# Keeping split expert weights on chip between the two expert stages of a macaron block

## What is computed

```
x = L0_attn_x
x = x + 0.5 * ffn(layernorm(x), router, gate, up, down)
x = x + attention(layernorm(x), W_qkv, W_out)      # rotary, causal, 16 heads
x = x + 0.5 * ffn(layernorm(x), router, gate, up, down)

ffn(x):   top 2 of 8 experts by x @ router.T, their logits through a softmax
          out = sum over the two e of weight_e * (silu(x @ gate[e].T) * (x @ up[e].T)) @ down[e].T
```

## Time and profile before

| | |
|---|---|
| median of 3 runs | 1350.76 us (1350.12 to 1356.05) |
| the profiled execution | 1353.68 us, its span 1351.6 us, mean granted clock 0.956 |
| f1 routing block | about 6 to 51 us |
| f1 expert block and attention | 51 to about 1059 us |
| f2 routing block | about 1060 to 1104 us |
| f2 expert block and final sum | 1104 to 1352 us |

### The profile page before, as it was taken

How to read it: one execution, slowest core, us unless ns; L and a number is a source line. 1 busy time by engine, 2 the same in 40 slices (tenths; PEclk the granted TensorE clock), 3 DMA queues, 4 the chain that set the end, 5 groups by cost and what they waited for, 6 DMA issues and landing times. The chain is left out here.

```text
span 1351.6 us, 27022 instructions
## 1 busy us (share of the span) xinstructions
PE 1232.3 (91%) x8148; PEld 906.6 (67%) x8148; DVE 934.7 (69%) x2002; ACT 785.9 (58%) x2230; POOL 848.0 (63%) x911
## 2 busy tenths in 40 slices
PE   7699999938999999999999999999998879999990
PEld 6488888825666666666666666666665658888880
DVE  5675333337888888888888888888887577533335
ACT  5455665515665666666666656656556455555552
POOL 4267776516767668677667677676665336766652
PEclk8799999967999999999999999999999889999995
DMA  9311111112212222221212222222111521111116
GB/s 306 113 40 45 47 48 46 40 51 58 55 46 48 64 48 48 63 48 47 56 42 63 48 48 64 48 47 48 45 42 26 180 84 41 44 48 49 46 40 190
DMA packets 86473, 86.44 MB, mean 64 GB/s; under 512 B 10496, under 2 KB 77056, under 8 KB 85824
## 3 DMA queue, kind: packets, MB, share of 16 engines
q1 hardware_dynamic: 73024, 63.99, 17.7%
q0 software_dynamic: 9088, 18.63, 4.9%
q10 hardware_dynamic: 4224, 2.10, 0.5%
HBM read 35.53 MB, written 15.60 MB: 38 GB/s over the span
## 5 line engine op out<-in xcount | busy, mean ns | idle before, releaser
L1382 POOL TENSOR_SCALAR at_prob<-at_prob,at_rec 128x128 f32<-128x128 f32 (+3 forms) x256 | 315.6, 1237 | 216.1 <-DVE at_rec L1554 215.0
L1638 ACT ACTIVATE at_prob<-at_s,at_nb 128x128 f32<-128x128 f32 (+3 forms) x512 | 265.4, 527 | 50.5 <-DVE at_nb L1546 45.9
L1647 ACT ACTIVATE at_probT<-at_pt 128x128 f32<-128x128 f32 (+3 forms) x256 | 105.0, 437 | 230.1 <-PE at_pt L1477 230.1
L1000 DVE TENSOR_TENSOR f_hid<-f_b,f_silu 128x512 f32<-128x512 f32 x142 | 98.1, 691 | 170.0 <-PE f_b L886 146.9
L1546 DVE TENSOR_REDUCE at_nb<-at_s 128x2 f32<-128x256 f32 (+3 forms) x256 | 208.8, 816 | 8.0 <-PE at_s L1463 8.0
L844 POOL DMA_INDIRECT f_xb<-xn_dram,f_source x142 | 147.7, 1040 | 87.6 <-issue 40.5
L853 POOL DMA_INDIRECT ys_dram<-f_y,f_target x142 | 139.8, 985 | 93.8 <-issue 58.8
L1477 PE MATMUL at_pt<-ident,at_prob 128*128 128x128 f32 x1280 | 184.4, 275 | 1.8 <-DVE at_prob L1557 1.2
L1458 PE MATMUL at_s<-at_KT,at_QT 64*128 64x128 f32 (+3 forms) x1024 | 175.3, 461 | 5.0 <-DMA at_KT<-at_R 3.7
L1376 POOL TENSOR_TENSOR at_R<-at_turned 128x512 f32<-128x512 f32 x128 | 159.3, 1263 | 30.4 <-DVE at_turned L1540 30.4
L1540 DVE TENSOR_TENSOR at_turned<-at_pj,rope 128x1024 f32<-128x1024 f32 x122 | 148.9, 1221 | 40.3 <-PE at_pj L1424 40.3
(11 more groups left out here) (261 smaller groups left out, 2152.0 us busy)
## 6 DMA issues: line engine op xcount, KB each, us to landing
at_QT<-at_R SPq DMA_DIRECT2D x128, 128.0 KB, 2.4
at_KT<-at_R SPq DMA_DIRECT2D x128, 128.0 KB, 2.3
f_gate<-gate_t SPq DMA_DIRECT2D x16, 256.0 KB, 4.9
f_up<-up_t SPq DMA_DIRECT2D x16, 256.0 KB, 6.6
xn_dram<-f_xn SPq DMA_DIRECT2D x16, 256.0 KB, 4.4
f_down<-down_t SPq DMA_DIRECT2D x2, 2048.0 KB, 8.0
at_got<-ys_dram SPq DMA_DIRECT2D x16, 256.0 KB, 3.3
f_got<-ys_dram SPq DMA_DIRECT2D x16, 256.0 KB, 5.1
```

The source lines that it names most:

```text
L1382: pool.tensor_scalar(w, w, rec[:, q, 1:2], None, ALU.mult).then_inc(probB_ready, 1)
L1638: act.activation(prob[q][:, h, :], s_bank[q % 2][:, h, 0:n], ACT.Exp, bias=nb[:, q, h:h + 1], scale=1.0, accum_out=sums[:, q, h:h + 1]).th ...
```

## The change

- The hi and lo tiles of gate and the hi tile of up become tiles of `macaron` and live through both stages. The lo tile of up stays per stage; f1 writes it to DRAM (`up_lo_dram`, 2 MB) and f2 reads it back.
- f2 (SPLITS false) loads no gate or up and splits nothing: SP issues one DMA for up's lo. PE, ACT and SP keep the rest of the routing block.
- In f1 the store of up's lo is SP's first DMA of the expert block, ahead of the attention's weights. SP waits for it at the end of the block.
- POOL no longer subtracts pieces, in either stage. All 16 go through PE and ACT in f1.
- Of each lead group ACT normalises tiles 0 and 1, POOL tiles 2 and 3, in both stages. `turn` and SP's stores wait for both.
- The order in the loops changes: n runs from 2 to 15; on PE turn(g + 1), judge(g), trailing(n); on ACT turned(g), trailing(n), leading(n + 2). ACT's token products move to n = 8, its copy of the logits to n = 10, and PE's find to n = 10 to 13, one part in each round.

```diff
+        F = gate_t.shape[2]
+        gate = [sb(f"gate{z}", [P, E, F], F32R) for z in range(2)]
+        up_hi = sb("up_hi", [P, E, F], F32R)
+        up_lo_dram = nc.dram_tensor("up_lo_dram", (P, E, F), F32).ap()
...
+    SPLITS = gate_t is not None
...
+        up = [up_hi, sb("up1", [P, E, F], F32R)]
...
-        POOLED = range(PIECES - 5, PIECES)
-        TENSOR = PIECES - len(POOLED)
-        ORDER = [0, 1, POOLED[0], 2, POOLED[1], 3, *POOLED[2:], *range(4, TENSOR)]
...
                 def _(sp):
                     sp.dma_start(router[:, :], router_t).then_inc(w_in, 16)
-                    for n in range(PIECES):
+                    if not SPLITS:
+                        sp.dma_start(up[1][:, :, :].bitcast(F32), up_lo_dram).then_inc(up_lo_moved, 16)
+                    for n in range(PIECES if SPLITS else 0):
...
                         if g < LEAD_GROUPS:
                             sp.wait_ge(xn_ready, g + 1)
-                        else:
-                            sp.wait_ge(xn_ready_pool, g - LEAD_GROUPS + 1)
+                        sp.wait_ge(xn_ready_pool, g + 1)
...
                 def _(pool):
-                    pool.wait_ge(moments.shift_ready, 2)
-                    for g in range(LEAD_GROUPS, GROUPS):
-                        for n in range(4 * g, 4 * g + 4):
+                    for g in range(GROUPS):
+                        pool.wait_ge(moments.shift_ready, 1 if g < LEAD_GROUPS else 2)
+                        for n in range(4 * g + (2 if g < LEAD_GROUPS else 0), 4 * g + 4):
...
-                    for m, n in enumerate(POOLED):
-                        hi, lo = piece(n)
-                        pool.wait_ge(w_hi, ORDER.index(n) + 1)
-                        pool.tensor_tensor(lo, lo.bitcast(F32), hi.bitcast(F32), ALU.subtract
-                                           ).then_inc(w_lo_pool, 1)
...
                     def normed(g):
-                        for t in range(4):
+                        for t in range(2):
...
+                    if SPLITS:
+                        leading(0)
+                        leading(1)
+                        trailing(0)
+                        leading(2)
+                        trailing(1)
+                        leading(3)
+                    for n in range(2, PIECES):
+                        if LEAD_GROUPS + n - 2 < GROUPS:
+                            turned(LEAD_GROUPS + n - 2)
+                        if SPLITS:
+                            trailing(n)
+                            if n + 2 < PIECES:
+                                leading(n + 2)
+                        if n == 8:
+                            for k in range(2):
+                                routing.token_numbered(act, 0, k)
+                        if n == 10:
                             act.wait_ge(lg_psum, GROUPS)
...
-                    trailing(0)
-                    trailing(1)
+                    if SPLITS:
+                        trailing(0)
+                        trailing(1)
                     turn(LEAD_GROUPS)
-                    turn(LEAD_GROUPS + 1)
                     routing.count_tokens(pe, 0, bank[6][:, 0:LEAD * E], bank[7][:, 0:LEAD * E])
-                    for n in range(2, TENSOR):
-                        trailing(n)
+                    for n in range(2, PIECES):
+                        if LEAD_GROUPS + n - 1 < GROUPS:
+                            turn(LEAD_GROUPS + n - 1)
                         if LEAD_GROUPS + n - 2 < GROUPS:
                             judge(LEAD_GROUPS + n - 2)
-                        if n >= 3 and LEAD_GROUPS + n - 1 < GROUPS:
-                            turn(LEAD_GROUPS + n - 1)
-                    for c in range(4):
-                        routing.find(pe, 0, c, bank[6][:, 0:2 * routing.most])
+                        if SPLITS:
+                            trailing(n)
+                        if 10 <= n < 14:
+                            routing.find(pe, 0, n - 10, bank[6][:, 0:2 * routing.most])
...
                 def _(sp):
+                    sp.dma_start(up_lo_dram, up[1][:, :, :].bitcast(F32)).then_inc(up_lo_moved, 16)
                     sp.dma_start(w_all[:, 0:QK], w_qk).then_inc(all_in, 16)
```

More of the change, by code:

```diff
@@ L559, in ffn @@
         moments = Moments(nc, name, ctx, X, stats, mean, rstd, tmpa, tmpb, NB)
-        gate = [sb(f"gate{z}", [P, E, F], F32R) for z in range(2)]
-        up = [sb(f"up{z}", [P, E, F], F32R) for z in range(2)]
+        up = [up_hi, sb("up1", [P, E, F], F32R)]
         down = sb("down", [P, E, FC, P])
@@ L566, in ffn @@
         down_in = sem("down_in")
-        w_hi = sem("w_hi")
-        w_lo = sem("w_lo")
-        w_lo_pool = sem("w_lo_pool")
-        w_part = [sem(f"w_part{s}") for s in range(2)]
-        lo_psum = sem("lo_psum")
+        up_lo_moved = sem("up_lo_moved")
+        if SPLITS:
+            w_hi = sem("w_hi")
+            w_lo = sem("w_lo")
+            w_part = [sem(f"w_part{s}") for s in range(2)]
+            lo_psum = sem("lo_psum")
         xn_ready = sem("xn_ready")
@@ L696, in _ @@
                             moments.by_act(act, 1, LEAD, NB)
-                    leading(0)
-                    leading(1)
-                    trailing(0)
-                    leading(POOLED[0])
-                    leading(2)
-                    trailing(1)
-                    leading(POOLED[1])
-                    leading(3)
-                    for m in range(2, len(POOLED)):
-                        leading(POOLED[m])
-                    turned(LEAD_GROUPS)
-                    turned(LEAD_GROUPS + 1)
-                    for n in range(2, TENSOR):
-                        trailing(n)
-                        if n + 2 < TENSOR:
-                            leading(n + 2)
-                        if n >= 3 and LEAD_GROUPS + n - 1 < GROUPS:
-                            turned(LEAD_GROUPS + n - 1)
-                        if n == TENSOR - 3:
+                    if SPLITS:
[16 more added lines that the diff above has]
+                        if n == 10:
                             act.wait_ge(lg_psum, GROUPS)
@@ L718, in _ @@
                                            bank[3][:, 0:(NB - LEAD) * E], ACT.Copy).then_inc(logits_ready, 1)
-                            for k in range(2):
-                                routing.token_numbered(act, 0, k)
-                    act.wait_ge(w_lo, TENSOR)
+                    if SPLITS:
+                        act.wait_ge(w_lo, PIECES)
                 @block.tensor
@@ L727, in turn @@
                             pe.wait_ge(xn_ready, g + 1)
-                        else:
-                            pe.wait_ge(xn_ready_pool, g - LEAD_GROUPS + 1)
+                        pe.wait_ge(xn_ready_pool, g + 1)
                         wait(pe, xts_ready, g - 1)
@@ L838, in _ @@
                     sp.wait_ge(all_in, 64)
+                    sp.wait_ge(up_lo_moved, 16)
             @block.gpsimd
```

16 lines of the change are left out of this document (6 added, 10 removed).

## The result

The changed kernel took a median of 1358.70 us in ten runs (1356.51 to 1360.43). The kernel before took 1352.72 us in ten runs beside it (1350.12 to 1356.05). The kernel before spreads over 6 us in this set and over 5, 17 and 7 us in the three sets of experiments, so each experiment is given as a ratio to the kernel before beside it. In the second and third set of experiments the kernel before took 1413 and 1418 us, so between sets only ratios are compared. One variant ran in the first and in the third set, with the same text and on the same chip by its recorded number: its span is 1345.0 us in one and 1409.9 us in the other.

A forecast was written before the change was run, and what follows sets the result against it. The prediction took TensorE to bound the long stages (PE 91% busy) and the last-ending engine chain each routing block. Terms +6.5 + 4 - 5.7 = +4.8 us, on the median 1350.76, gave 1355.6 us; range 1348 to 1363.

The forecast's parts named there:

- The first block, +6.5: First stage's routing block: more pieces on ACT and PE and a new loop order lengthen it by 6.5 us.
- the ring: First stage's loop: turned, judge and trailing wait for each other; three rounds of 3.75 us, not 2.4, cost +4.1 us.
- the old stall: First stage's loop: the wait on ACT's five casts and two copies behind L680 goes, -3.3 us.
- rival 1: First block +10 as the clock falls in its rounds, gathers wait behind the store +5.4: 1360.5 us, chance 0.24.
- The start of the expert loop, +4: First stage's first gathers: 2 MB store queued ahead of attention weights delays PE's projecting by 4 us, ends 0 and 8.
- The second block, -5.7: Second stage's routing block: contention and lead gains less a clock loss, -5.7 us, bounds -3 and -9.
- (a): Second stage's routing block: without POOL's subtractions DVE is no longer held up, -4.6 us.
- (b): Second stage's lead groups: POOL shares normalising, so the last judgements end 1.5 us earlier; 3.5 at PE's higher clock.
- (c): Second stage's routing block: PE nearly idle, so last find and count may run at low clock, +0.4 us.
- Rival 2: First block loses only a few pieces, ACT running ahead enough that no ring closes: +0.4, 1351.2 us, chance 0.20.
- rival 3: Faster: little first-block loss, higher PE clock in both lead phases, gathers pass the store: -5.2, 1345.6 us, chance 0.06.
- rival 4: Second stage withholds its gain because something else ends last there: +8.5, 1359.3 us, chance 0.10.

The follow-up runs named there:

- old order, 16 pieces: Changed kernel with the first stage's routing loops back in the previous order, all 16 pieces still on PE and ACT: 1349.42 us, ratio 0.9964 to the kernel before.
- filled ring: Changed kernel with eight idle PE transposes ahead of each of judgements 5 to 7 in the first stage: ratio 1.0026 to the kernel before.
- two stores: Changed kernel with up's lo stored twice to DRAM, both ahead of the attention's weights: 1353.57 us in one execution.
- changed again: The changed kernel unaltered, run once more beside later experiments: ratio 1.0039 to the kernel before.
- subtractions back: Changed kernel with five idle 128x512 POOL subtractions added in the second stage after POOL's tiles: 1364.82 us in one execution.
- the first block as before: Changed kernel with the first stage's routing block as in the kernel before, store of up's lo kept: 1347.80 us, ratio 0.9959; 0.9958 in a later set.

## Why the prediction was right, and where it was not

The time forecast was 1355.6 us, in a range of 1348 to 1363; it is 1358.7. That is inside the range but above the band that the forecast gave itself (1352.5 to 1357.5, chance 0.40), and above the 1357.5 us that it called slower. That line was drawn from a base of 1350.76 us; from the ten runs' base, 1352.72, it would be 1359.5, and the kernel is under it. The steps:

**The first block, +6.5.** Its terms can be read from the starts of the pieces. L761's third piece (n = 2) starts at 30.07 before, L758's at 28.30 after: -1.8, where the prediction let the lead phase's 1.5 us go into slow pieces, 0. From there to n = 6 it is 41.86 - 30.07 = 11.8 before and 43.35 - 28.30 = 15.1 after: +3.3, where the ring less the old stall was put at 4.1 - 3.3 = +0.8. From n = 6 to the block's end it is 9.0 before and 15.7 after: +6.7, where the five pieces, the find matmuls and the token products gave 6.4 - 2 + 1.5 = +5.9. Sum +8.2.

| | n = 2 at | to n = 6 | to the end | block's end |
|---|---|---|---|---|
| before | 30.07 | 11.8 | 9.0 | 50.88 |
| after | 28.30 | 15.1 | 15.7 | 59.05 |
| old order, 16 pieces | 30.28 | 7.9 | 14.3 | 52.43 |
| filled ring | 28.68 | 13.0 | 15.4 | 57.03 |

The mechanism was right: the ring is there, with 3.94 us for the forecast 3.75. The term that failed is the clock's. It had been kept out of the forecast as rival 1, with the argument that the second stage had gone through a similar gap at full clock; in after the ring's last round and the piece behind it run slow. At full clock (filled ring) the middle column is +1.2 to before, close to the +0.8. The price that the prediction gave a slow round, about 2 us, is its upper end: slow rounds took 4.76 to 5.90 us, 0.8 to 2.0 over 3.94. So the first half of rival 1 is nearly true: the block ended at 58.61, 59.05, 61.18 and 62.95 us in four profiled executions of the same block (two stores, after, changed again, subtractions back), +7.7 to +12.1 over the kernel before, where the forecast was +6.5 and the rival +10. This fits that the medians differ by more than the two traces. What takes the clock down in one execution after 34 us and in another after 38 is not settled: the filled ring had 1.00 and the old order did, one execution of each, but the kernel before had 0.68 in 34 to 38 us, behind its own wait of 1.19 us for the first turned group (the prediction called it a gap of about 2 us), and the variant with the old loops and the shared lead, in the longest of its executions, had this (stretches, columns as above):

```profile
30.00:34.00 4.00, 4.00 (x18) 3.21 (x16) 3.79 (x7) 1.72 (x4) 2.78 (x3) 0.61 0.94 393
34.00:38.00 4.00, 4.00 (x15) 3.17 (x15) 3.56 (x14) 1.42 (x3) 0.00 (x0) 0.50 0.02 8
```

So the clock falls in some executions of the old order too. Counted over the traces, the mean granted clock from 30 to 48 us is 0.81, 0.81, 0.81, 0.72 and 0.63 in the five executions with the unfilled ring, and 1.00, 1.00, 0.99, 0.91, 0.91, 0.91 and 0.62 in the seven with the old order. The ring's clock was lower as a rule and not always, so a part of the clock's loss, but no fixed number of microseconds, belongs to the ring.

**The start of the expert loop, +4.** This step failed too. It measured +0.7, of which 9.71 - 9.38 = 0.3 lie in the gathers. The price per megabyte was worked out from two points, 9.4 us with 3 MB and 4.05 us with none, by a straight line through them. Two stores show that there is no line: 9.1 us with 7 MB. What counts is whether there are bulk transfers beside a gather, and hardly how many. The lower end of that term, 0, was the nearer one.

**The second block, -5.7.** Measured -6.3, and each part of it as put: (a) contention -4.45 by the same two operations, for -4.6; (b) lead -2.0, for -1.5; (c) from sizes to source list 14.56 us for 14.33, +0.2, for +0.4. The subtractions put back gave +4.4.

Term (b) was worked out for PE at the lower clock, with 3.5 us if it kept the higher one. Both occur. In eight of the eleven traces with a shared lead the logits came 16.49 to 17.54 us after the block's start. In three (two stores, changed again, and the first block as before in its later set) it was 14.64 to 14.93 us, 3.7 to 4.0 less than the 18.59 of before.

One reading was off without effect on the sum: DVE's 1.68 us for "both" don't fall beside the four subtractions, which start behind it, but beside the fifth, which started at 1081.97. On the rule of the Trainium skill ("SBUF — State Buffer", Who interferes with whom), that a DVE instruction with two SBUF inputs is held by a GpSimd instruction that reads SBUF: the trace agrees where POOL subtracts (0.69 to 1.71 us for "both"). L349, which has one input, was held as well (0.17 to 1.23 us), so this rule alone does not cover all four. Where POOL normalises tiles of 128 elements in the lead phase the price is small, L321's 0.42 us beside its 0.29, and the 0 that was taken came out: from the logits to "both" DVE took 3.77 us before and 3.75 us after.

**The sum.** +8.2 + 0.7 + 0.2 - 6.3 = +2.8 in the profiled executions, for +4.8: the first block was put too low by 1.7, the store too high by 3.3. With the mean of the four block ends, 60.4, the first block is +9.6, 3.1 above its term, and the two errors cancel: +9.6 + 0.7 + 0.2 - 6.3 = +4.2. The medians show +6.0. The 1.8 us between +4.2 and +6.0 are not accounted for. The 3.1 us between forecast and result are 1.2 us of difference (6.0 for 4.8) and 2.0 us of the base: the forecast stood on the median of three runs, 1350.76, and that of ten is 1352.72. That the total came this close is luck: its terms missed by more.

**The rivals.** Rival 1's first half is there, with +9.6 in the mean of four traces for its +10; its second half (gathers behind the store) is not. Rival 2, a hidden ring, and rival 3, a gain, are refuted by the rounds of 3.94 us, though two of rival 3's terms came, the gathers passing the store nearly freely (+0.7 in all) and, in three of eleven traces, the second stage's lead at the higher clock; rival 4 by DVE's times in f2, since nothing else took its place at the end.

## What to carry to other kernels

When two in-order engines share a loop, write down what each step waits for and follow it once round: with the same work in the same engines, the order trailing, judge, turn took 2.4 us a round and the order turn, judge, trailing 3.9 us. A change that saves work in one stage and loosens an order in another should be split into these two, and the order be put back: here it turned +0.4% into -0.4%. When a change of a few microseconds leaves an engine waiting, read several traces of the same kernel before the clock is given a price: here one block's end moved over 4.3 us between them. Price a contention of transfers by its presence first, not by its bytes, and start the small transfers that the first matmul waits for ahead of the bulk ones.

## What the runs showed of the hardware

- Indirect gathers of 128 rows beside large plain transfers: the second transpose came 9.4, 9.7 and 9.1 us after the first gather's issue with 3, 5 and 7 MB issued beside them (9.55 to 10.32 us in ten executions with 5 MB), 4.0 us with none beside in the second stage, and 5.5 us with the bulk held back in the first.
- In a loop in which PE was busy for 60 to 69% the granted clock fell from 1.00 to 0.50, in some executions after two rounds and in others after one. It fell in four of seven executions of the old order too, between 30 and 48 us. Four executions of one and the same routing block ended at 58.61, 59.05, 61.18 and 62.95 us. With idle transposes in the gaps the clock was 1.00 in the one execution that was profiled.
- The second stage's lead phase, the same work each time, took 14.64 to 14.93 us in three executions and 16.49 to 17.54 us in eight. In 9 to 13 us from its start the granted clock was 1.00 in one of the short ones and 0.50 in one of the long ones.
- Five POOL subtractions of 128 x 512 (6.64 us) lengthened four DVE operations beside them by 4.0 us, among them one of 128 x 8 from 0.17 to 1.23 us.
